# Causal attention's result as one single precision tile, its projection as four products a group, and the experts' loop written out

## The reference, cut to what matters

```python
ln1_out = _layernorm(hidden_states, ln1_weight, ln1_bias)
qkv = jnp.einsum('sbh,oh->sbo', ln1_out, qkv_weight)
...
attn = jnp.einsum('bhst,tbhd->sbhd', probs, v).reshape(S, B, H)
proj_out = jnp.einsum('sbh,oh->sbo', attn, proj_weight)
hidden_after_attn = hidden_states + proj_out
ln2_out = _layernorm(hidden_after_attn, ln2_weight, ln2_bias)
...
gate = jax.nn.softmax(logits, axis=-1)
top_probs, top_idx = jax.lax.top_k(gate, TOP_K)
h_mid = jax.nn.gelu(jnp.einsum('th,ehf->etf', x, moe_w1))
expert_out = jnp.einsum('etf,efh->eth', h_mid, moe_w2)
...
return hidden_after_attn + moe_out
```

## Time and profile before

| | |
|---|---|
| median of 3 runs | 936.9 us (935.6 to 938.14) |
| the profiled execution's own time | 936.91 us |
| its span, first to last instruction | 934.9 us |
| TensorE matmul busy | 748.2 us, 80% of the span |
| VectorE busy | 659.0 us, 70% |
| ScalarE busy | 394.8 us, 42% |
| GpSimd busy | 217.2 us, 23% |
| mean granted TensorE clock | 0.897 of full speed |

### The profile page before, as it was taken

How to read it: one execution, slowest core, us unless ns; L and a number is a source line. 1 busy time by engine, 2 the same in 40 slices (tenths; PEclk the granted TensorE clock), 3 DMA queues, 4 the chain that set the end, 5 groups by cost and what they waited for, 6 DMA issues and landing times. The chain is left out here.

```text
span 934.9 us, 26246 instructions
## 1 busy us (share of the span) xinstructions
PE 748.2 (80%) x10100; PEld 554.6 (59%) x10100; DVE 659.0 (70%) x1809; ACT 394.8 (42%) x746; POOL 217.2 (23%) x334
## 2 busy tenths in 40 slices
PE   2579889888728787787888747787774999999998
PEld 1345556555516666665667525565553888888886
DVE  4478878886445888888888657787665666666653
ACT  2122222221122445555555535566542555455553
POOL 4333333331081221133010054244001111111100
PEclk9558888987955999999999958999996999999999
DMA  3000000420113012211220000000000000000000
GB/s 95 20 20 13 18 11 20 124 46 9 16 30 99 29 55 72 73 29 53 75 72 14 13 3 4 4 5 5 4 5 2 1 13 11 11 11 11 11 12 12
DMA packets 33081, 26.41 MB, mean 28 GB/s; under 512 B 9740, under 2 KB 29912, under 8 KB 32984
## 3 DMA queue, kind: packets, MB, share of 16 engines
q1 hardware_dynamic: 29944, 24.07, 9.7%
q10 hardware_dynamic: 3040, 0.98, 0.4%
HBM read 13.51 MB, written 7.34 MB: 22 GB/s over the span
## 5 line engine op out<-in xcount | busy, mean ns | idle before, releaser
L1736 PEld LDWEIGHTS bank<-w2r,hme 128*128 128x128 f32 x1024 | 132.5, 192 | 15.8 <-ACT hme L1590 1.4
L1736 PE MATMUL bank<-w2r,hme 128*128 128x128 f32 x1024 | 135.8, 276 | 0.0
L1590 ACT ACTIVATE hme<-bank,b 128x512 f32<-128x512 f32 x128 | 86.5, 687 | 96.4 <-PE bank L97 96.3
L792 ACT ACTIVATE P<-bank 128x512 f32<-128x512 f32 x128 | 76.6, 598 | 95.4 <-PE bank L985 95.4
L1687 DVE SCALAR_TENSOR_TENSOR Xq<-bank,wgte,Xq 128x128 f32 (+1 forms) x256 | 72.0, 343 | 51.9 <-PE bank L1736 38.4
L915 DVE TENSOR_SCALAR bank<-bank 128x512 f32<-128x512 f32 x128 | 89.0, 695 | 25.0 <-PE bank L976 24.9
L923 DVE TENSOR_REDUCE mx<-bank 128x4 f32<-128x512 f32 x128 | 86.9, 680 | 1.5 <-PE bank L968 1.4
L985 PE MATMUL bank<-mT,negsel 128*128 128x128 f16 x512 | 50.6, 222 | 44.4 <-DVE bank L915 41.7
L350 ACT ACTIVATE sg<-bank 128x512 f32<-128x512 f32 x40 | 23.9, 597 | 127.9 <-PE bank L581 100.2
L985 PEld LDWEIGHTS bank<-mT,negsel 128*128 128x128 f16 x512 | 31.9, 98 | 55.5 <-issue 40.6
L592 PE MATMUL bank<-w_raw,hm 128*128 128x128 f32 x320 | 50.4, 309 | 4.5 <-DVE X L506 4.5
(11 more groups left out here) (372 smaller groups left out, 1740.1 us busy)
## 6 DMA issues: line engine op xcount, KB each, us to landing
cross_q<-qh SPq DMA_DIRECT2D x24, 128.0 KB
K<-cross_k SPq DMA_DIRECT2D x96, 32.0 KB
Q<-cross_q SPq DMA_DIRECT2D x8, 384.0 KB, 3.4
X<-in_x SPq DMA_DIRECT2D x8, 256.0 KB, 2.8
Xq<-X SPq DMA_DIRECT2D x32, 64.0 KB
cross_k<-kh SPq DMA_DIRECT2D x16, 128.0 KB
Yq<-Y SPq DMA_DIRECT2D x32, 64.0 KB
out_x<-Xq SPq DMA_DIRECT2D x32, 64.0 KB, 1.7
```

The costliest lines, as they stand in the source:

```text
L792: act.activation(P[j][:], TB[j % 2][:], ACT.Exp, scale=SCALE).then_inc(s["p_ready"], 1)
L1590: act.activation(hm[:, p % HR], UP[p % RING][:], ACT.Gelu_apprx_tanh, bias=b1[:, p:p + 1]).then_inc(s["gelu"], 1)
L1736: last = pe.matmul(Y[e % 2][:, cols], hm[:, p % HR, cols], w2r[:, p], start=(p % 2 == 0 and i == 0), stop=(p % 2 == 1), skip_group_check=True)
```

## The change

The result of causal attention is kept as one single precision tile `AT` of 128 x 4096 instead of two 16 bit halves, and so is the weight `wp`. ScalarE writes `AT` at k = 2 instead of k = 3, and VectorE's L1379 and L1307 are gone. The projection of a group is four single precision products instead of twelve of halves. The loop over groups in `experts1` is written out on all four engines. Line numbers behind the change are up to five lower than before.

```diff
@@ attention2
         s = room.sems("""raw wT_ready pwp_ready pT stack hi lo bias b8_ready fixed summed
...
-            s_psum s_max m_hi m_lo mT_psum mT_ready t_psum p_ready v_psum v_ready pv_done o_sb dd_inv dd_hi dd_lo r_psum at_f at_hi at_lo""")
+            s_psum s_max m_hi m_lo mT_psum mT_ready t_psum p_ready v_psum v_ready pv_done o_sb dd_inv dd_hi dd_lo r_psum at_f at_done""")
...
                 act.wait_ge(s["pT"], 1)
-                act.activation(wp[0][:], bank[1][:, 0:128], ACT.Copy).then_inc(s["hi"], 1)
+                act.activation(wp[:], bank[1][:, 0:128], ACT.Copy).then_inc(s["hi"], 1)
...
-                    if k == 3 and chunk(n - 1):
+                    if k == 2 and chunk(n - 1):
                         act.wait_ge(s["at_f"], n)
-                        act.activation(tok(AT[0], n - 1), Af[:], ACT.Identity, bias=bv[:]).then_inc(s["at_hi"], 1)
+                        act.activation(tok(AT, n - 1), Af[:], ACT.Identity, bias=bv[:]).then_inc(s["at_done"], 1)
...
                 dve.wait_ge(s["hi"], 1)
-                dve.tensor_tensor(wp[1][:], bank[1][:, 0:128], wp[0][:], ALU.subtract)
...
                     if k == 1 and chunk(n - 1):
                         dve.wait_ge(s["r_psum"], n)
                         dve.wait_ge(s["o_sb"], n)
-                        after(dve, s["at_lo"], n - 1)
+                        after(dve, s["at_done"], n - 1)
                         dve.tensor_tensor(Af[:], Of[:], RB[:], ALU.mult).then_inc(s["at_f"], 1)
-                    if k == 3 and chunk(n - 1):
-                        dve.wait_ge(s["at_hi"], n)
-                        dve.scalar_tensor_tensor(tok(AT[1], n - 1), Af[:], bv[:], tok(AT[0], n - 1),
-                                                 ALU.add, ALU.subtract).then_inc(s["at_lo"], 1)
@@ experts1, the same on POOL, ACT, DVE and PE
-                over_groups(pe, step, -1, G - 1)
+                for g in range(-1, G):
+                    step(g)
@@ experts1, PE
                     if p == 0:
                         after(pe, s["xTe_lo"], g)
                         for i in range(GB):
-                            last = split_product(pe, PX[:, 128 * i:128 * i + 128], [tok(t, g, 128 * i, 128) for t in AT],
-                                                 [w[:] for w in wp])
+                            last = pe.matmul(PX[:, 128 * i:128 * i + 128], tok(AT, g, 128 * i, 128), wp[:],
+                                             start=True, stop=True)
                         last.then_inc(s["pj_psum"], 1)
@@ build
-        AT = [room.sb(f"AT{i}", [C, S * B], F16) for i in range(2)]
-        wp = [room.sb(f"wp{i}", [C, C], F16) for i in range(2)]
+        AT = room.sb("AT", [C, S * B])
+        wp = room.sb("wp", [C, C])
```

More of the change, by code:

```diff
@@ L1579, in step @@
                                                ).then_inc(s["r_ready"], 1)
-                over_groups(pool, step, -1, G - 1)
+                for g in range(-1, G):
+                    step(g)
             @block.scalar
@@ L1598, in step @@
                                            ACT.Exp).then_inc(s["g_exp"], 1)
-                over_groups(act, step, -1, G - 1)
+                for g in range(-1, G):
+                    step(g)
             @block.vector
@@ L1695, in step @@
                             prep(g + 1, p)
-                over_groups(dve, step, -1, G - 1)
+                for g in range(-1, G):
+                    step(g)
                 for e in (NE - 2, NE - 1):
```

## The result

The changed kernel takes 939.18 us (median of 20 runs, 934.29 to 944.06), the kernel before 933.63 us in as many runs beside it (929.33 to 938.88). The ratio is 1.0061, with a 95% interval of 1.0041 to 1.008: slower by about 5 us. The predicted 938.5 us and the range held, but the side did not: the forecast was "no change", and the change costs more than that. The predicted difference was +1.6 us, the measured one is 5.5 us.

A forecast was written before the change was run, and what follows sets the result against it. TensorE was taken to bound the experts' stage, with no engine full in the causal stage. Terms 1.0 + 1.0 - 0.8 - 0.2 + 0.6 = +1.6 us on 936.9 gave 938.5 us; 8 in 10 range 934.8 to 941.2.

The forecast's parts named there:

- the write: Causal stage: the write at k = 2 delays `mc` by 0.62 us in six chunks, mostly swallowed by instruction waits; +0.6 us.
- The experts' stage: TensorE is full there, so dearer single precision projections count: +1.0 us at full clock and +1.0 us at clock 0.50.
- The six blocks at full clock: Experts' stage, six groups: each block with a projection grows 0.16 us, from 2.26 to 2.42; together +1.0 us.
- The two projections at the lower clock: First and second groups' projections, at granted clock 0.50: 0.5 us more each, together +1.0 us.
- The loop written out: Experts' stage: VectorE's 1.05 us after a jump back is covered by full TensorE, so removing the jumps brings 0.
- The seam: Last chunk to first projection: without VectorE's low half, TensorE starts at 708.94 instead of 709.72; -0.8 us.
- The start's: Start of the causal stage: L1307 no longer holds VectorE ahead of the half weights TensorE's transposes need; -0.2 us.
- first rival: Causal stage: the moved write is not swallowed, TensorE's fetch wait moves along; 2.5 instead of 0.6, 940.4 us, chance 0.17.
- VectorE was not the bound: Causal stage: L1379's 0.74 us buys nothing; the rival that VectorE was the bound gave -4.2 us, 932.7, chance 0.07.

The follow-up runs named there:

- unroll_only: The kernel before with only the loops of the experts' stage written out: 933.38 us, ratio 1.0015.
- after_third: The changed kernel unaltered, timed again in the third series on its own chip: 939.74 us, ratio 1.0064 to the kernel before.
- before_again: The kernel before unaltered, timed again against itself: 932.23 us, ratio 0.9973.
- after_again: The changed kernel unaltered, timed again in the first series: 936.76 us, ratio 1.0052 to the kernel before.
- before_k2: The kernel before with only ScalarE's write of the high half moved from k = 3 to k = 2: 937.09 us, ratio 1.0018.

## Why the time was predicted right and the change was not

**The number.** That 938.5 us came so close to the measured 939.18 is luck. The sum starts from 936.9 us, the median of the three runs known then, and the median of twenty is 933.63: 3.3 us too high. The change that it adds is +1.6 us where 5.5 were measured: 3.9 us too small. The two errors cancel. More than half of the second, 2.4 us, is one term, the write.

**The experts' stage.** Price and place were right. The six blocks at full clock measured 0.16 us each, as in the sum. The two projections at the lower clock grew by 0.6 us (706.16 to 708.32, against 1.55 between the same rows before) and 0.42 (forecast 0.5 each). In the profiled pair the stage is 1.1 us longer, over the traces 1.6 (226.4 in the seven with single precision, 224.8 in the five with halves throughout), against the +2.0 of the sum.

**The loop written out** was priced at 0, and `unroll_only` shows it. VectorE had its 1.05 us, TensorE nothing, and their going changed no time. The rule of the Trainium skill's page "Runtime: NRT & Kernel Launch" (Instruction fetch mechanics) on taken branches agrees with the row of VectorE and not with TensorE's.

**The seam** gave its 0.8 us at its own place. In this pair they were lost within the same 8 us to a longer wait for instructions and an earlier fall of the clock. Whether that belongs to the change or to these two executions is open. **The start's** 0.2 us is not resolved: the first `mc` stands 26.6 to 26.9 us behind the stage's start in the traces of either form.

**The write of `AT` at k = 2 is the step that failed.** The mechanism was the one described, and the delay even a little larger (0.75 us where 0.62 was forecast; 0.32 to 0.76 over the six chunks). What was wrong was the term's size: +0.6 us in the sum, 3.0 us in the runs. I let TensorE's waits for instructions swallow three and a half of the six delays. They mostly moved along instead. In the profiled pair, counted from each stage's start, the `mc` of k = 0 behind chunk 1 comes 0.99 us later than in the kernel before, of which 0.27 are given back at k = 1. In the chunks 2, 3 and 4 0.2 to 0.3 us stay each (forecast 0.15), in chunk 6 0.4. Only in chunk 5 are the 1.75 us of the earlier trace rows gone, and 0.7 us come back. There the changed kernel's clock was halved (first line), and TensorE came to the end of its instructions later. In `after_third`, which had the full clock at this place, the wait stands (second line). So this pair does not show that the delay was swallowed. Over chunks 1 to 6 these waits add up to 8.5 to 11.9 us in the four traces with the write at the end of k = 3, and to 6.2 to 8.7 us in the four with the write at the end of k = 2. So some of them did shorten; how much of that the lower clock did is open.

```profile
666.00:669.30 3.30, 3.30 (x108) 2.73 (x109) 1.04 (x3) 1.08 (x2) 0.00 (x0) 0.50 0.02 5
```

```profile
676.20 0.23 PE L1432 MATMUL bank<-Pd,Vq 128*32 128x32 f32 x3 [1.48 <-issue]
```

That is the first rival's mechanism, and its net 2.5 us for the write, 940.4 us with a chance of 0.17, was the better reading. The range, too, counted the write at 0 to 1.5 us, where the term's own bound was 3.7. The Trainium skill's same section ("Runtime: NRT & Kernel Launch", Instruction fetch mechanics) has the sequencer fetch the next page while it executes the current one; by that every delay ahead of a wait would have been swallowed and the write would have cost 0.3 us, and the runs with the write at k = 2 do not agree.

The delays themselves account for a part of the 3.0 us only. Two pairs of traces have the same mean clock in the causal stage, before and the changed kernel (0.99) and `before_again` and `after_again` (0.97). From chunk 1 to the stage's last `mc` the changed kernel loses 1.25 and 1.1 us there; without what chunk 5 gave back, the first pair would have 2.0. The rest may be the lower clock inside the causal stage, which no case of mine had there. The traces with the write at k = 2 have a mean clock of 0.94, 0.94, 0.96, 0.97 and 0.99 in it, the nine others 0.97 to 1.00. That the longer idle times bring the lower clock fits this, but identical programs differ as much (0.99 and 0.94). The clock of whole runs speaks for it in one kernel and against it in the other. Where it is on record, its mean is 0.916 with halves and the write at k = 3 (129 runs) and 0.911 for the changed kernel (44), but 0.915 for `before_k2`, which lost the same 3.0 us. What lowers it is not settled.

**VectorE was not the bound**, as judged: it lost 0.74 us a chunk and waited 6 us longer.

**The forecast said itself what would refute it**: a causal stage changed by over 1.5 us. The profiled pair changed by 1.1. Only the mean over the traces goes beyond: 173.2 us for the three of the changed kernel, against 170.5 for before, `before_again` and `unroll_only`. The difference of 2.7 hangs on `after_third` with its 175.9 us and has an uncertainty of 1.5. That 2.7 and the experts' 1.4 of the same traces (226.35 against 224.95) make 4.1 us; the times say 939.0 - 933.8 = 5.2, with an uncertainty of 0.5.

## What to carry to other kernels

Put a write that nobody waits for behind the step for which the others wait, and in a place where its own input is long ready: an engine's idle time is free only if it is not idle for that input. Do not count on a wait for instructions as a cushion: here it mostly moved along with the engine that waited. And price an edit of a few tenths of a us in a repeated step by the distance between two repeated rows at full clock; here that distance agreed to 0.01 us from trace to trace, while whole spans differed by 1%.

## What the runs showed of the chip that I had not expected

The first part of the program, identical in all fourteen traces, took 533.7 to 539.3 us. Inside the causal stage the granted clock of one and the same kernel was 0.99 in one execution and 0.94 in another. Here are short stretches of `after_third` within it, where TensorE is at work and the clock is halved nonetheless:

```profile
636.00:640.00 4.00, 3.98 (x133) 3.09 (x131) 1.95 (x6) 1.35 (x3) 1.04 (x1) 0.57 0.01 4
```

```profile
677.00:681.00 4.00, 3.78 (x18) 1.66 (x15) 2.29 (x6) 1.06 (x3) 0.00 (x0) 0.57 0.02 4
```

TensorE is busy for 3.98 and 3.78 of 4 us there. With some 13 us more at half clock than in the first trace, the stage is 3.7 us longer, about 0.3 us for each. With the first part's 5.6 us from shortest to longest, this is of the size of the scatter between runs of one kernel (8 to 10 us from shortest to longest in each set, a standard deviation of 2.4 to 4.1). What lowers the clock in one execution and not in the next no run here shows.
